# Layer 1 scan: products in place in three PSUM bank pairs, tables built on three engines

## What is computed

```python
def step(s, inp):
    k_l, v_l, w_l, r_l = inp
    a = k_l[..., :, None] * v_l[..., None, :]
    out = jnp.einsum('bhs,bhst->bht', r_l, faaaa * a + s)
    s_new = a + w_l[..., None] * s
    return (s_new, out)
```

## Time and profile before

| | us |
|---|---|
| three runs | 3399.28, 3405.37, 3408.23 |
| their median | 3405.37 |
| the profiled execution | 3410.99 |
| its span, first to last instruction | 3408.9 |
| outside the span | 2.1 |
| mean granted TensorE clock | 0.948 of full |
| scan phase, from its barrier to the last copy of `ps_y` | about 749.5 to 970.3 |

### The profile page before, as it was taken

One profiled execution on the slowest core, in us unless ns is written; L12 is line 12 of the kernel. 1 busy time (PEld: TensorE's weight loads), 2 busy tenths in 40 slices (PEclk: granted clock), 3 DMA queues, 4 the chain that ended last, 5 costly groups with the idle time before them and its releaser, 6 DMA issues. The chain is left out here.

```text
span 3408.9 us, 47898 instructions
## 1 busy us (share of the span) xinstructions
PE 3079.6 (90%) x17313; PEld 2567.3 (75%) x17313; DVE 1912.0 (56%) x3919; ACT 1470.1 (43%) x3387; POOL 863.1 (25%) x880
## 2 busy tenths in 40 slices
PE   5999898987778789999999988999999997989997
PEld 4777497544434589989999888998989986955663
DVE  2444533328863466665566666666566555147774
ACT  2444442220011244455544644446554464246771
POOL 0222400305541321132011431104101041055632
PEclk9999999988898899999999999999999998988997
DMA  4131020100001320114101241012401023021110
GB/s 125 65 98 40 26 75 6 56 16 0 0 0 37 98 80 27 46 53 130 52 27 46 71 145 45 28 45 76 132 27 53 20 82 102 1 75 39 58 23 20
DMA packets 131964, 182.75 MB, mean 54 GB/s; under 512 B 17743, under 2 KB 99548, under 8 KB 131740
## 3 DMA queue, kind: packets, MB, share of 16 engines
q1 hardware_dynamic: 119012, 143.96, 13.7%
q0 software_dynamic: 12544, 35.77, 3.4%
q10 hardware_dynamic: 184, 0.05, 0.0%
HBM read 165.88 MB, written 13.86 MB: 53 GB/s over the span
## 5 line engine op out<-in xcount | busy, mean ns | idle before, releaser
L71 PE MATMUL l2a<-l_arena,l_arena 128*128 128x400 f32 (+2 forms) x1856 | 652.1, 351 | 34.5 <-DVE l_arena L2724 14.7
L72 PE MATMUL l2a<-l_arena,l_arena 128*128 128x400 f32 (+2 forms) x1856 | 632.7, 341 | 0.0
L73 PE MATMUL l2a<-l_arena,l_arena 128*128 128x400 f32 (+2 forms) x1856 | 632.6, 341 | 0.0
L71 PEld LDWEIGHTS l2a<-l_arena,l_arena 128*128 128x128 f32 (+1 forms) x1856 | 352.4, 190 | 56.8 <-issue 47.0
L72 PEld LDWEIGHTS l2a<-l_arena,l_arena 128*128 128x128 f32 (+1 forms) x1856 | 354.0, 191 | 2.7
L73 PEld LDWEIGHTS l2a<-l_arena,l_arena 128*128 128x128 f32 (+1 forms) x1856 | 352.6, 190 | 2.0
L2589 ACT ACTIVATE l_arena<-l2a 121x384 fp32r<-121x384 f32 (+1 forms) x208 | 99.6, 479 | 442.5 <-PE l2a L2364 442.5
L2384 PE MATMUL l2a<-l_arena,l_arena 121*128 121x384 f32 (+1 forms) x768 | 279.4, 364 | 3.2 <-DVE l_arena L2790 3.2
L2386 PE MATMUL l2a<-l_arena,l_arena 121*128 121x384 f32 (+1 forms) x768 | 264.0, 344 | 0.0
L2385 PE MATMUL l2a<-l_arena,l_arena 121*128 121x384 f32 (+1 forms) x768 | 263.3, 343 | 0.0
L2239 POOL DMA_DIRECT2D p_dram_layer<-l_arena x128 | 62.7, 495 | 726.1 <-DVE l_arena L2790 724.4
(11 more groups left out here) (427 smaller groups left out, 6918.1 us busy)
## 6 DMA issues: line engine op xcount, KB each, us to landing
l_arena<-in_L_xattn_wq_dram SPq DMA_DIRECT2D x32, 512.0 KB, 3.5
l_arena<-in_L_xattn_wk_dram SPq DMA_DIRECT2D x32, 512.0 KB, 5.0
l_arena<-in_L_xattn_wv_dram SPq DMA_DIRECT2D x32, 512.0 KB, 3.5
l_arena<-in_L_xattn_wo_dram SPq DMA_DIRECT2D x64, 256.0 KB, 2.7
l_arena<-ctxT_hi POOLq DMA_DIRECT2D x16, 724.0 KB, 4.6
l_arena<-ctxT_lo POOLq DMA_DIRECT2D x16, 724.0 KB, 6.1
l0mlp_staged<-in_L_xattn_mlp_w_dram SPq DMA_DIRECT2D x16, 512.0 KB, 4.1
l2mlp_staged<-in_L_xattn_w_fc_dram SPq DMA_DIRECT2D x16, 512.0 KB, 4.2
```

Of the source, the lines that this page charges most:

```text
L71: pe.matmul(out, cut_a(a.hi), cut_b(b.hi), start=start, stop=False)
L72: pe.matmul(out, cut_a(a.hi), cut_b(b.lo), start=False, stop=False)
L73: return pe.matmul(out, cut_a(a.lo), cut_b(b.hi), start=False, stop=stop)
```

## The change

`ps_v` goes. There are three pairs of banks `ps_kv[0..2]`, and the spread writes straight into the pair in the 101-column layout; the key multiplies there in place. For that v is stored in the same layout with zeros in column 0, and the four matmuls of a spread have 512, 296, 512 and 296 columns. Pairs go to steps by the list BANKS, which is 0, 1, 2 repeated five times and then 1 for step 15. A spread waits for the last scan that used its pair (`last_in_banks`), a key waits only for its spread. The tables are built on three engines: `gather` on GpSimd, even spread tables on VectorE, odd ones on ScalarE. The core of the diff:

```diff
+    BANKS = [0, 1, 2] * 5 + [1]
+    PIECES = (slice(0, 512), slice(512, B * PREV))
+
+    def last_in_banks(t):
+
+        return max(u for u in range(t - N1, t) if BANKS[u % N1] == BANKS[t])
+
...
-        v = Split(own, nc, "v_split", [P, KT, B * L])
+        v = Split(own, nc, "v_split", [P, KT, B, PREV])
...
-        ps_v = own.enter_context(nc.psum_tensor("ps_v", [P, HALVES, 512], F32))
-        ps_kv = [own.enter_context(nc.psum_tensor(f"ps_kv{i}", [P, 1024], F32)) for i in range(2)]
+        ps_kv = [own.enter_context(nc.psum_tensor(f"ps_kv{i}", [P, 1024], F32)) for i in range(3)]
...
             k.sems.clear_ended(pool)
+            pool.memset(gather[:], 0.0).then_inc(blank, 1)
+            for part in (v.hi, v.lo):
+                last = pool.memset(part[:, :, :, 0].bitcast(F32), 0.0)
+            last.then_inc(v_padded, 1)
+            pool.wait_ge(blank, 1)
+            pool.wait_ge(built, 2)
+            for t in range(N1):
+                last = pool.tensor_copy(gather[:, t, t:P:N1], k.same_head[:, t:P:N1])
+            last.then_inc(gather_built, 1)
...
-            dve.tensor_reduce(k.head_of[:], ident, AX.X, ALU.add)
-            dve.memset(gather[:], 0.0).then_inc(built, 1)
+            dve.tensor_reduce(k.head_of[:], ident, AX.X, ALU.add).then_inc(built, 1)
...
-            dve.wait_ge(built, 2)
-            for t in range(N1):
-                dve.tensor_scalar(spread[:, t, :], k.same_head[:], rows[:, t:t + 1], None, ALU.mult)
-                last = dve.tensor_copy(gather[:, t, t:P:N1], k.same_head[:, t:P:N1])
-            last.then_inc(built, 1)
             for t in range(KT):
                 dve.wait_ge(v_rounded, t + 1)
-                v.rest(dve, lambda x: x[:, t, :], T["v"][:, t, :]).then_inc(v_split, 1)
+                v.rest(dve, lambda x: x[:, t, :, 1:PREV], by_batch(T["v"][:, t, :])).then_inc(v_split, 1)
+            dve.wait_ge(built, 2)
+            for t in range(0, N1, 2):
+                last = dve.tensor_scalar(spread[:, t, :], k.same_head[:], rows[:, t:t + 1], None, ALU.mult)
+            last.then_inc(spread_dve, 1)
             with dve.Fori(0, KT) as m:
                 for t in range(N1 + 1):
                     if t < N1:
                         dve.wait_ge(spreaded, at(m, N1, t))
-                        dve.wait_ge(scanned, at(m, N1, t - 2))
-                        dve.tensor_tensor(
-                            kv[t % 2][:, :, 1:PREV].rearrange("p (h b) l -> p h b l", h=HALVES),
-                            ps_v[:, :, 0:HALF].rearrange("p h (b l) -> p h b l", l=L),
-                            T["k"][:, bass.ds(m, 1), :].squeeze(1).rearrange("p (h b l) -> p h b l", h=HALVES, l=L),
-                            ALU.mult).then_inc(keyed, 1)
+                        spread_v = kv[BANKS[t]][:, :, 1:PREV]
+                        dve.tensor_tensor(spread_v, spread_v, by_batch(T["k"][:, bass.ds(m, 1), :].squeeze(1)),
+                                          ALU.mult).then_inc(keyed, 1)
...
+            act.wait_ge(built, 2)
+            for t in range(1, N1, 2):
+                last = act.activation(spread[:, t, :], k.same_head[:], ACT.Copy, scale=rows[:, t:t + 1])
+            last.then_inc(spread_act, 1)
...
-            pe.wait_ge(built, 3)
             pe.wait_ge(v_split, KT)
+            pe.wait_ge(v_padded, 1)
+            pe.wait_ge(spread_dve, 1)
+            pe.wait_ge(spread_act, 1)
+            pe.wait_ge(gather_built, 1)
             with pe.Fori(0, KT) as m:
                 for t in range(N1 + GATHER):
                     if t < N1:
-                        pe.wait_ge(keyed, at(m, N1, t - 1))
+                        pe.wait_ge(scanned, at(m, N1, last_in_banks(t)))
```

More of the change, by code:

```diff
@@ L1492, in layer1_scan @@
         built = sem("l1s_built")
+        spread_dve, spread_act = sem("l1s_spread_dve"), sem("l1s_spread_act")
+        blank, gather_built = sem("l1s_gather_blank"), sem("l1s_gather_built")
         spreaded = sem("l1s_spread")
@@ L1502, in layer1_scan @@
         v_split = sem("l1s_v_split")
+        v_padded = sem("l1s_v_padded")
         block = own.enter_context(nc.Block())
@@ L1563, in _ @@
                             T["w"][:, bass.ds(m, 1), :, :].squeeze(1).rearrange("p b l -> p (b l)"),
-                            ps_kv[u % 2][:, 0:B * PREV], 0.0, ALU.mult, ALU.add).then_inc(scanned, 1)
+                            ps_kv[BANKS[u]][:, 0:B * PREV], 0.0, ALU.mult, ALU.add).then_inc(scanned, 1)
         @block.scalar
@@ L1571, in _ @@
             for t in range(KT):
[L1572 removed]
+                v.round(act, lambda x: x[:, t, :, 1:PREV], by_batch(T["v"][:, t, :])).then_inc(v_rounded, 1)
+            act.wait_ge(built, 2)
+            for t in range(1, N1, 2):
+                last = act.activation(spread[:, t, :], k.same_head[:], ACT.Copy, scale=rows[:, t:t + 1])
+            last.then_inc(spread_act, 1)
             act.wait_ge(loaded, 16 * B)
@@ L1578, in _ @@
                     act.wait_ge(keyed, at(m, N1, t))
-                    act.activation(kv[t % 2][:, :, 0], start[:, bass.ds(m, 1), :, t].squeeze(1), ACT.Copy
+                    act.activation(kv[BANKS[t]][:, :, 0], start[:, bass.ds(m, 1), :, t].squeeze(1), ACT.Copy
                                    ).then_inc(started, 1)
@@ L1593, in _ @@
                     if t < N1:
-                        pe.wait_ge(keyed, at(m, N1, t - 1))
+                        pe.wait_ge(scanned, at(m, N1, last_in_banks(t)))
                         for part in (v.hi, v.lo):
-                            for half in range(HALVES):
-                                mm = pe.matmul(ps_v[:, half, 0:HALF], spread[:, t, :],
-                                               part[:, bass.ds(m, 1), half * HALF:(half + 1) * HALF].squeeze(1),
+                            flat = part[:].rearrange("p m b l -> p m (b l)")
+                            for piece in PIECES:
+                                mm = pe.matmul(ps_kv[BANKS[t]][:, piece], spread[:, t, :],
+                                               flat[:, bass.ds(m, 1), piece].squeeze(1),
                                                start=(part is v.hi), stop=(part is v.lo))
```

## The result

| | before | changed |
|---|---|---|
| median of six runs, us | 3405.2 (3399.3 to 3408.5) | 3380.1 (3376.9 to 3392.1) |
| ratio | | 0.9936, 95% interval 0.992 to 0.9951 |
| profiled execution, us | 3411.0 | 3380.6 |
| mean granted TensorE clock of it | 0.948 | 0.957 |
| scan phase, VectorE's first operation to its first of the next phase, us | 221.0 (749.60 to 970.61) | 202.3 (750.28 to 952.55) |

The kernel is faster by 0.64%, 21.8 us by the ratio. The phase that the change touches gives 18.7 of it in these two profiles.

A forecast was written before the change was run, and what follows sets the result against it. VectorE was taken to bound the scan phase. Blocks 11.0, stalls 1.3 and tables 3.5 us saved make 15.8, from 3410.99 to 3395.2 for the profiled execution, 3389.6 as median; range 3382 to 3401.

The forecast's parts named there:

- What bounds the phase: Scan phase: VectorE sets the pace, with uncounted gaps of 0.20 us; a block falls by 2.75 us to 48.01.
- No wait on the previous scan: Steps key(1) to key(14): 2.64 us each instead of 2.84, saving 2.60 us a block.
- Three pairs: Block start: spread(1) runs right behind spread(0), so key(1) follows key(0) by 0.95 us, not 2.09; saves 1.14 a block.
- BANKS: Step 15: spread(15) must wait for scan(13), so key(15) follows key(14) by 3.83 us, not 2.84; costs 0.99 a block.
- The stalls: Few steps into each block, key waits on half-clock TensorE: 0.6 us each, 2.4 in place of 3.7, saving 1.3.
- In place: Key reading and writing the same bank still takes 1.00 us; upper bound 2.00 us.
- The rival of a slow bank: Every key lengthens if a bank cannot be read and written at one go; at 2.00 us, 3453.6 us; chance 0.06.
- The tables: Before the loop: tables built on three engines let TensorE's first spread start 3.5 us earlier.
- the two ways that I had as bounds: GpSimd's table copies: no interference with VectorE, 4.4 us saved, or all 16 shutting VectorE out in turn, 0.6 saved.
- The sum: Blocks 11.0, stalls 1.3 and tables 3.5 us make 15.8 us saved.
- The signs: Would make the forecast wrong: other key length, 0.50 clock beyond step 6, copies well over 0.24 us, changed time outside the phase.
- my low end of 3382: Whole kernel: 19.1 us saved with tables 4.4 and no stalls, and runs some 4 us about their median.

The follow-up runs named there:

- seamless: Changed kernel with its four blocks written out instead of looped, pairs running on as g mod 3; ratio 0.9907 to the kernel before, phase 182.3 us.
- second: Changed kernel profiled again without any edit; ratio 0.9939 to the kernel before, scan phase 204.1 us.
- third: Changed kernel profiled once more without any edit, one run; scan phase 204.2 us.

## Why the prediction was right, point by point

- **What bounds the phase.** VectorE, by its own operations and by small gaps that the view of waits leaves out. It held: the block that the starts add up to, 48.0 us, came out as 48.0, 47.7 and 47.7, and with the waits at the block ends taken away (seamless) the loop is VectorE's 2.62 us a step and nearly nothing else.
- **No wait on the previous scan.** Right in mechanism and size: 2.62 for 2.64, shown by putting the wait back. The Trainium skill (page "VectorE: DVE Perf Modes", section "The DRAIN you can't avoid") says that VectorE operations chained without semaphores are no faster, from copies with a semaphore after each or only after the last. That doesn't carry over to a key behind a scan: here a wait for the operation just ahead costs 0.2 us.
- **Three pairs.** Right: key(1) follows by 0.91 (0.95), and without the third pair a step costs 3.84. In the first block it was 2.79 before and 1.23 after, at half clock, where the sum had 2.09 and 0.95 for all four.
- **BANKS.** Right: 3.80 (3.83) at step 15, gone with the entry changed. In the last block it was 4.51, and in the other two profiles it was 4.1 to 4.5 in three blocks of four. I had not seen this: TensorE stands idle for 2.9 us ahead of every spread(15), and in some blocks the granted clock then falls to half (0.50 from 940.0 to 946.6). The last block saved 2.0 us and the others 3.9 to 4.6, because spread(15) and the gathers behind it, up to 946.6, ran at half clock:

```profile
940.66 1.04 PE L1618 MATMUL ps_kv<-v_split_hi,spread 128*128 x2 [2.90 <-DVE state L1574]
941.50 0.88 PE L1618 MATMUL ps_kv<-v_split_lo,spread 128*128 x2
942.17 9.13 PE L1628 MATMUL ps_y<-rs,gather 128*128 128x400 f32 x20
```

- **The stalls.** Mis-sized. I took 0.6 each, 2.4 in all. In the first profile there were none, in the other two 0.66, 0.44 and 0.10 (second, 1.2 in all) and nearly the same (third). The clock still falls there; the spell was over sooner than I let it last, and the spread that runs a step ahead covered it. One stretch of the changed kernel's second block shows it, columns as in the earlier trace rows:

```profile
813.80:817.20 3.40, 3.40 (x9) 2.36 (x9) 3.40 (x4) 0.19 (x1) 2.42 (x2) 0.53 0.00 0
```

Half clock nearly throughout, TensorE busy all the time, and VectorE too. Before, the same part of a block had VectorE busy 4.42 of 5.00. The length of a spell shows in the third block, first before, then with the change:

```profile
870.90:881.10 10.20, 7.64 (x19) 5.23 (x18) 9.52 (x7) 0.56 (x3) 5.51 (x4) 0.50 0.00 0
```

```profile
861.40:864.80 3.40, 3.32 (x7) 2.34 (x8) 3.40 (x4) 0.19 (x1) 2.33 (x2) 0.50 0.00 0
```

How much of this is the third pair's is only partly shown: the tables alone took 2.7 us of the stalls away, with half-clock spells as long as before (10.2 us in the third block). In the kernel with the wait put back, which has tables and third pair, the fifth key is at most 0.04 us late.

- **In place.** Right, 1.00 us at a key that waited, in place as across banks. The rival of a slow bank is out.
- **The tables.** 4.15 where I had 3.5. GpSimd's start and the clearing came as worked out (751.0 in a phase that began 0.7 later, 1.83 us). The copies behaved in neither of the two ways that I had as bounds: the ones beside VectorE waited, up to 0.96 us, but VectorE did not, and those that ran alone cost 0.13 from start to start and not the 0.235 of my row for 32 columns. The Trainium skill's exclusive lock (page "SBUF — State Buffer", section "SBUF: two separate sides") would have either side wait, whichever starts second. The trace agrees for GpSimd alone: `rest` operations that start while a copy runs take 0.98 us, as without one.
- **The sum.** 15.8 us for the phase; 18.7, 16.9 and 16.8 were measured. Term by term, us saved:

| | forecast | first profile | second |
|---|---|---|---|
| up to key(0) (tables) | 3.5 | 4.2 | 4.2 |
| key(0) to key(1) | 4.6 | 5.1 | 5.1 |
| 13 steps a block | 10.4 | 11.0 | 11.0 |
| stalls | 1.3 | 3.6 | 2.4 |
| step 15 | -4.0 | -4.6 | -5.6 |
| key(15) to the next key(0), and to the end | 0 | -0.7 | -0.2 |
| sum | 15.8 | 18.7 | 16.9 |

  Four terms came out better than forecast and two worse, so the errors partly cancel.
- **The signs.** Some that I had set down as making the forecast wrong appeared, and the total stood all the same: copies on GpSimd took 0.96 and 0.26 us, over the 0.24, and still GpSimd, the last of the three, was done 6.9 us into the phase (VectorE 6.2, ScalarE 5.5), where VectorE alone had taken 11.0; the clock was at 0.50 beyond step 6, at step 15; and the time outside the phase changed by 12.1 us between the first profiles, which the repeats don't confirm.
- **The range.** The changed kernel's median of 3380.1 lies 1.9 us under my low end of 3382; by the ratio it is 3383.4, inside. The low end rested on runs lying some 4 us about their median. They spread more, 3374 to 3393 in the changed kernel's thirteen runs, while the phase differs by only 1.9 us in three profiles; the forecast should have had the rest of the kernel as a term. Of the 21.8 us by which the whole time moved, the phase gives 16.8 to 18.7. The others are neither forecast nor explained.

## What to carry to other kernels

Look at the starts of instructions and not only at waits: an operation held for the end of the one just ahead of it on its engine loses 0.2 us here, the view of waits shows nothing, and one more buffer takes the wait away. When buffers rotate in a loop whose length they don't divide, one step reuses a buffer too early, and it pays to work out which step, what is queued behind it, and whether the loop can be written out. Judge an edit of under 1% by the length of its own phase in several profiles, since what lies behind it differs here by up to 20 us from profile to profile.

## What the runs showed of the hardware that I had not expected

- GpSimd's copies of 128 x 8 take 0.20 us alone, 0.26 beside VectorE's one-input fp32 tables, and up to 0.96 beside its subtractions with two SBUF inputs (L58), with VectorE not slowed.
- TensorE's mean granted clock over layer 3's attention, which no edit touches, was 0.89 to 0.95 from profile to profile, and the stage lasted 311 to 295 us. Why the spells differ is left open.
- The same small stalls come back almost to the hundredth in two profiles of one kernel (0.66, 0.44, 0.10 and 0.66, 0.48, 0.11) and not in the first of it. What sets the pattern was not settled.
